# A two-layer selective scan on one core: first batch's softplus ahead of the last projections, dt out of PSUM ahead of the convolution

## The reference

```python
h = _layernorm(x) * (1 + ca) + sa
x = x + ga * attn(h)          # block 0: additive attention; block 1: two selective-scan layers
h = _layernorm(x) * (1 + cb) + sb
x = x + gb * ffn(h)           # block 0: FP4-quantised gated FFN; block 1: expert-choice mixture of experts
```

```python
xz = jnp.einsum('bld,ed->ble', x, W_in)
u, z = jnp.split(xz, 2, axis=-1)                     # 256 channels each
u = _silu(_causal_conv1d(u, conv_w, conv_b))         # 4 taps
x_dbl = jnp.einsum('bld,rd->blr', u, W_x)
dt, Bm, Cm = jnp.split(x_dbl, [8, 24], axis=-1)      # 8 | 16 | 16
dt = jax.nn.softplus(jnp.einsum('blr,dr->bld', dt, W_dt) + b_dt)
A = -jnp.exp(A_log)
y = _selective_scan(u, dt, A, Bm, Cm, Dvec)          # h = exp(dt A) h + dt B u, y = C h + D u, 16 states
y = y * _silu(z)
return jnp.einsum('bld,od->blo', y, W_out)
```

## Time and profile before

| what | value |
|---|---|
| median of 3 runs | 959.33 us (958.27 to 960.14) |
| profiled execution | 958.83 us, span 957.1 us |
| TensorE's mean granted clock | 0.831 of full |
| TensorE (PE) busy | 663.8 us, 69% |
| VectorE (DVE) busy | 677.4 us, 71% |
| ScalarE (ACT) busy | 439.1 us, 46% |
| GpSimd (POOL) busy | 567.0 us, 59% |
| decay Exp on ScalarE (L693), mean of one | 0.716 us |
| prologue of layer 0 | from 201.18 us (first projection) to 255.78 us (first scan) |
| prologue of layer 1 | from 485.19 us to 541.67 us |

### The profile page before, as it was taken

One profiled execution on the slowest core, in us unless ns is written; L12 is line 12 of the kernel. 1 busy time (PEld: TensorE's weight loads), 2 busy tenths in 40 slices (PEclk: granted clock), 3 DMA queues, 4 the chain that ended last, 5 costly groups with the idle time before them and its releaser, 6 DMA issues.

```text
span 957.1 us, 8556 instructions
## 1 busy us (share of the span) xinstructions
PE 663.8 (69%) x2416; PEld 337.7 (35%) x2416; DVE 677.4 (71%) x867; ACT 439.1 (46%) x715; POOL 567.0 (59%) x297
## 2 busy tenths in 40 slices
PE   3675576567377797878788386787978744299990
PEld 2344244432032232323322032232323224288880
DVE  6742477566598889899945598999998865844430
ACT  2413142257576465555556666465565513022220
POOL 6101564400399888999900399898998913136555
PEclk9755677688589899899997589899999975599995
DMA  4000000000000000000000000000000061012222
GB/s 154 0 1 1 0 1 0 1 0 0 1 0 0 1 0 0 0 0 0 0 1 0 1 0 1 0 0 1 0 0 0 0 241 44 1 12 19 20 21 22
DMA packets 11363, 13.05 MB, mean 14 GB/s; under 512 B 1545, under 2 KB 9914, under 8 KB 10690
## 3 DMA queue, kind: packets, MB, share of 16 engines
q1 hardware_dynamic: 6434, 10.51, 3.0%
q0 software_dynamic: 4896, 2.13, 2.6%
HBM read 8.43 MB, written 4.21 MB: 13 GB/s over the span
## 4 chain that ended last, share of the span: by engine, by line
PE 33%; DVE 29%; issue 14%; POOL 10%; ACT 9%; DMA 2%; DVEq 1%; POOLq 0%; ACTq 0%; SPq 0%
PE ps L924 7%; DVE ps L1302 6%; DVE hs_all L1315 6%; POOL hc_all L456 4%; PE ps L1050 3%; PE ps L1066 3%; PE ps L1027 2%; DVE w_ffn L1315 2%; PE ps L930 2%; ACT ps L693 2%; PE ps L886 2%; PE ps L769 1%; POOL dbu L443 1%; DVE big L1117 1%; DVE dbu L1349 1%
## 5 line engine op out<-in xcount | busy, mean ns | idle before, releaser
L924 PE MATMUL ps<-hc_all,ident 128*128 128x512 f32 x512 | 264.0, 640 | 21.6 <-POOL hc_all L456 20.4
L456 POOL TENSOR_TENSOR hc_all<-hs_all,c_row 128x1024 f32<-128x1024 f32 x88 | 210.5, 2392 | 19.4 <-DVE hs_all L1315 16.2
L690 ACT COPY c_row<-ps 128x512 f32<-128x512 f32 x128 | 74.9, 585 | 161.6 <-PE ps L943 145.9
L924 PEld LDWEIGHTS ps<-hc_all,ident 128*128 128x128 f32 x512 | 100.5, 201 | 119.1 <-issue 73.6
L1315 DVE TENSOR_TENSOR_SCAN hs_all<-da,ps 128x1024 f32<-128x1024 f32 x48 | 109.8, 2287 | 11.6 <-ACT da L693 5.4
L693 ACT ACTIVATE da<-big,a_neg 128x511 f32 (+1 forms) x176 | 117.2, 716 | 0.0
L1302 DVE TENSOR_TENSOR ps<-big,ps 128x1024 f32<-128x1024 f32 x88 | 107.4, 1220 | 11.7 <-POOL big L432 4.8
L456 POOL TENSOR_TENSOR hc_all<-w_ffn,c_row 128x1024 f32<-128x1024 f32 x40 | 94.2, 2356 | 22.1 <-DVE w_ffn L1315 22.1
L1315 DVE TENSOR_TENSOR_SCAN hs_all<-ps,dbu 128x1024 f32<-128x1024 f32 x40 | 91.0, 2274 | 12.4 <-POOL hc_all L456 9.7
L443 POOL TENSOR_TENSOR dbu<-big,w_mod 128x1024 f32<-128x1024 f32 x40 | 96.1, 2401 | 0.0
L1315 DVE TENSOR_TENSOR_SCAN w_ffn<-da,ps 128x1024 f32<-128x1024 f32 x40 | 91.5, 2287 | 5.3
(11 more groups left out here) (253 smaller groups left out, 1103.3 us busy)
## 6 DMA issues: line engine op xcount, KB each, us to landing
tmpA<-w_in SPq DMA_DIRECT2D x2, 1024.0 KB, 6.9
tmpB<-w_in SPq DMA_DIRECT2D x2, 1024.0 KB, 9.0
x_tok<-x_in SPq DMA_DIRECT2D x1, 1024.0 KB, 6.6
out<-x_tok SPq DMA_DIRECT2D x1, 1024.0 KB, 7.2
xm_rows<-xn SPq DMA_DIRECT2D x1, 1024.0 KB, 5.3
w_mod<-w_mod_in SPq DMA_DIRECT2D x1, 768.0 KB, 4.6
out<-hc_all,hs_all POOLq DMA_INDIRECT x40, 3.0
w_ffn<-w_ffn_in SPq DMA_DIRECT2D x1, 560.0 KB, 7.4
```

The source lines that it names most:

```text
L456: nc.gpsimd.tensor_tensor(hc[:, n % 4, :, :], hs3[HS_BUF[n]].rearrange("p (i s) -> p i s", i=IC), c_row[:, n % 4, :].unsqueeze(1).to_broad ...
L690: nc.scalar.copy(c_row[:, n % 4, :], ps[:, CB, :]).then_inc(c_cs, 1)
L924: mm = nc.tensor.matmul(ps[:, YS + i, :], ident[:], hc[:, n % 4, i, :], start=(n == 0), stop=(n == NS - 1))
```

## The change

The instructions and their shapes stay the same. Their order on three queues, the waits, and one bank pair change:

- VectorE: L1268 (dt out of PSUM) moves ahead of the convolution and counts `m_pos` for each half. In the last turn the sum of softplus of batch 0 (L1281) stands ahead of L1268 of batch 3.
- ScalarE: Abs (L659) moves ahead of z's Silu and waits half by half. In turn 4 the table load, A and Exp of batch 0 follow. In turn 5 Ln of batch 0 stands right after L629. The Silu load moves ahead of the hT writes (layer 0) and ahead of the last `store_h` of the layer before (layer 1).
- TensorE: batch 3's dt product goes into banks 0 and 1 and does not wait for Abs of batch 2. The waits ahead of the loop ask only for Abs of batches 0 to 2 and the rows of batch 0; the rest is asked for at state n = 3, ahead of the first product that writes banks 0 and 1. The first projection of layer 0 waits for two hT writes, and its z half for all four.

```diff
--- before.py
+++ after.py
@@ -168,7 +168,7 @@
         dtT = big[:, 0:IC * T].rearrange("p (b i s) -> p b i s", b=B, i=IC)
         dtuT = big[:, IC * T:2 * IC * T].rearrange("p (b i s) -> p b i s", b=B, i=IC)
         SP = S + KC - 1
-        XD, DTP = [4, 5], 6
+        XD, DTP = [4, 5], [6, 6, 6, 0]
         hs_all = sb("hs_all", [P, 2 * IC * S])
         hs = hs_all[:].rearrange("p (k i s) -> p k i s", k=2, i=IC)
         hc_all = sb("hc_all", [P, 4 * IC * S])
@@ -609,6 +609,7 @@
 
             act.wait_ge(stat_ready, 3 * NT)
             nc.scalar.activation(std[:], mv[:, :, 1], ACT.Sqrt, bias=eps[:, 0:1]).then_inc(std_ready, 1)
+            act.preload_act_table(ACT.Silu)
             for b in range(B):
                 act.wait_ge(norm_tr, B + b + 1)
                 nc.scalar.activation(hT[:, b * S:(b + 1) * S], ps[:, b, :], ACT.Identity, bias=mod_cols[:, 2, b:b + 1],
@@ -616,7 +617,14 @@
             for l in range(L):
                 q = sems[l]
 
-                act.preload_act_table(ACT.Silu)
+                def softplus_exp(b):
+                    act.wait_ge(q["m_abs"], b + 1)
+                    nc.scalar.activation(splus[:, b, :, :], splus[:, b, :, :], ACT.Exp, scale=-1.0).then_inc(q["m_ln"], 1)
+
+                def softplus_ln(b):
+                    act.wait_ge(q["m_ln"], 2 * b + 1)
+                    nc.scalar.activation(splus[:, b, :, :], splus[:, b, :, :], ACT.Ln, bias=1.0).then_inc(q["m_ln"], 1)
+
                 if l:
 
                     act.wait_ge(c_sum, NS * B)
@@ -627,6 +635,8 @@
                         after(act, q["m_dtp"], b - 2)
                         nc.scalar.copy(dt_low, ps[2 * NS:2 * NS + DR, XD[k], :]).then_inc(q["m_dtl"], 1)
                         nc.scalar.copy(bc_parts[0:2 * NS, b - 2, :], ps[0:2 * NS, XD[k], :]).then_inc(q["m_hi"], 1)
+                    if b == B + 1:
+                        softplus_ln(0)
                     if b < B:
 
                         act.wait_ge(q["m_in"], 2 * b + 1)
@@ -649,29 +659,24 @@
                             act.wait_ge(q["m_conv"], IC * (b - 1) + i + 1)
                             nc.scalar.activation(uT[:, b - 1, i, :], conv[:, (b - 1) % 2, i, :], ACT.Silu,
                                                  bias=vec(V_CB + l * IC + i)).then_inc(q["m_u"], 1)
+                    if b >= 2:
+
+                        for i in range(IC):
+                            act.wait_ge(q["m_pos"], IC * (b - 2) + i + 1)
+                            ins = nc.scalar.activation(splus[:, b - 2, i, :], ps[:, DTP[b - 2] + i, :], ACT.Abs,
+                                                       bias=vec(V_BDT + l * IC + i))
+                        ins.then_inc(q["m_abs"], 1)
                     if b < B:
                         act.wait_ge(q["m_in"], 2 * b + 2)
                         nc.scalar.activation(zT[:, b, :, :], ps[:, 2:4, :], ACT.Silu).then_inc(q["m_z"], 1)
-                    if b >= 2:
-
-                        act.wait_ge(q["m_pos"], b - 1)
-                        for i in range(IC):
-                            ins = nc.scalar.activation(splus[:, b - 2, i, :], ps[:, DTP + i, :], ACT.Abs,
-                                                       bias=vec(V_BDT + l * IC + i))
-                        ins.then_inc(q["m_abs"], 1)
-                act.preload_act_table_set("natural_log_exp_and_others")
-                if l == 0:
-
-                    nc.scalar.activation(a_neg[:].rearrange("p l i n -> p (l i n)"), vec(V_AL, L * IC * NS),
-                                         ACT.Exp).then_inc(a_exp, 1)
-
-                def softplus_log(b):
-                    act.wait_ge(q["m_abs"], b + 1)
-                    nc.scalar.activation(splus[:, b, :, :], splus[:, b, :, :], ACT.Exp, scale=-1.0).then_inc(q["m_ln"], 1)
-                    act.wait_ge(q["m_ln"], 2 * b + 1)
-                    nc.scalar.activation(splus[:, b, :, :], splus[:, b, :, :], ACT.Ln, bias=1.0).then_inc(q["m_ln"], 1)
-
-                softplus_log(0)
+                    if b == B:
+
+                        act.preload_act_table_set("natural_log_exp_and_others")
+                        if l == 0:
+                            nc.scalar.activation(a_neg[:].rearrange("p l i n -> p (l i n)"), vec(V_AL, L * IC * NS),
+                                                 ACT.Exp).then_inc(a_exp, 1)
+                        softplus_exp(0)
+
                 act.wait_ge(decay_zero, l + 2)
                 act.wait_ge(a_ready, 1)
                 def store_h(b):
@@ -700,7 +705,10 @@
                         if n == OUT_AT + 1 and not isinstance(b, int):
                             store_h(b)
                         if isinstance(b, int) and n + 2 in DT_AT:
-                            softplus_log(1 + DT_AT.index(n + 2))
+                            softplus_exp(1 + DT_AT.index(n + 2))
+                            softplus_ln(1 + DT_AT.index(n + 2))
+                if l + 1 < L:
+                    act.preload_act_table(ACT.Silu)
                 store_h(B)
 
             act.wait_ge(stat_ready, 4 * NT)
@@ -871,7 +879,6 @@
                     mm = nc.tensor.transpose(ps[:, b, j * P:(j + 1) * P], xn[:, b * TB + j, :], ident[:])
                 mm.then_inc(norm_tr, 1)
             pe.wait_ge(ld_mamba, 64)
-            pe.wait_ge(hT_ready, 2 * B)
             pe.wait_ge(consts, 7)
             for l in range(L):
                 q = sems[l]
@@ -881,6 +888,8 @@
 
                     if l:
                         pe.wait_ge(c_h, b + 1)
+                    elif b == 0:
+                        pe.wait_ge(hT_ready, B + 2 * (half + 1))
                     after(pe, q[["m_u0", "m_z"][half]], [2, 1][half] * b)
                     for i in range(IC):
                         mm = nc.tensor.matmul(ps[:, 2 * half + i, :], w_in[:, l, (2 * half + i) * P:(2 * half + i + 1) * P],
@@ -891,9 +900,10 @@
                 for b in range(B + 2):
                     if b >= 2:
                         pe.wait_ge(q["m_dtl"], b - 1)
-                        after(pe, q["m_abs"], b - 2)
+                        if b < B + 1:
+                            after(pe, q["m_abs"], b - 2)
                         for i in range(IC):
-                            mm = nc.tensor.matmul(ps[:, DTP + i, :], w_dt[:, l, i * P:(i + 1) * P], dt_low,
+                            mm = nc.tensor.matmul(ps[:, DTP[b - 2] + i, :], w_dt[:, l, i * P:(i + 1) * P], dt_low,
                                                   start=True, stop=True)
                         mm.then_inc(q["m_dtp"], 1)
                     if b < B:
@@ -909,8 +919,8 @@
                             mm = nc.tensor.matmul(ps[0:DR + 2 * NS, XD[(b - 1) % 2], :], w_x[:, l, i, :], uT[:, b - 1, i, :],
                                                   start=(i == 0), stop=(i == IC - 1))
                         mm.then_inc(q["m_xd"], 1)
-                pe.wait_ge(q["m_abs"], B)
-                pe.wait_ge(q["m_lo"], B)
+                pe.wait_ge(q["m_abs"], B - 1)
+                pe.wait_ge(q["m_lo"], 1)
 
                 def add_skip(b):
 
@@ -962,6 +972,9 @@
                         if n == LAG:
 
                             after(pe, c_y, l * B + b)
+                            if isinstance(b, int):
+                                pe.wait_ge(q["m_abs"], B)
+                                pe.wait_ge(q["m_lo"], B)
                         if n >= LAG:
                             add_state(at - LAG, n - LAG)
                         elif not isinstance(b, int):
@@ -1236,6 +1249,11 @@
             normalise(3)
             for l in range(L):
                 q = sems[l]
+                def softplus(b):
+                    dve.wait_ge(q["m_ln"], 2 * b + 2)
+                    dve.wait_ge(q["m_pos"], IC * (b + 1))
+                    v.tensor_tensor(dtT[:, b, :, :], dtT[:, b, :, :], splus[:, b, :, :], ALU.add).then_inc(q["m_dt"], 1)
+
                 if l:
                     dve.wait_ge(c_scan, B * NS)
                 v.memset(u_pad[:, :, :, 0:KC - 1], 0.0).then_inc(pad_ready, 1)
@@ -1247,6 +1265,15 @@
                         after(dve, q["m_lo"], b - 3)
                         v.tensor_tensor(bc_rest[:, k, :], ps[0:2 * NS, XD[k], :], bc_parts[0:2 * NS, b - 2, :],
                                         ALU.subtract).then_inc(q["m_r1"], 1)
+                        if b == B + 1:
+                            if l == 0:
+                                dve.wait_ge(a_exp, 1)
+                                v.tensor_scalar(a_neg[:], a_neg[:], -1.0, None, ALU.mult).then_inc(a_ready, 1)
+                            softplus(0)
+                        dve.wait_ge(q["m_dtp"], b - 1)
+                        for i in range(IC):
+                            v.tensor_scalar(dtT[:, b - 2, i, :], ps[:, DTP[b - 2] + i, :], vec(V_BDT + l * IC + i), 0.0,
+                                            ALU.add, ALU.max).then_inc(q["m_pos"], 1)
                     if b < B:
 
                         dve.wait_ge(q["m_u0"], 2 * b + 2)
```

(16 more changed lines are left out.)

## The result

The changed kernel takes 935.89 us (median of 4 runs, 934.05 to 936.44), the kernel before 959.44 in the runs beside it (4 runs, 958.27 to 960.14). The ratio is 0.9754, with a 95% interval of 0.9740 to 0.9769: 23.5 us faster. Predicted were 940.0 us and a range of 936 to 946.

The account below looks back on a forecast made before the run. Each prologue delays the whole span; ScalarE's queue, held by VectorE's, sets its turns, and its end is serial. Layer 0's 10.2 us (0.75 + 4.0 + 5.5) and layer 1's 9.3 sum to 19.5, giving 940 us, range 936 to 946.

Parts of the forecast that it names:

- Start: Start of each layer's prologue, earlier first projection and hoisted Silu load: 0.75 us won in layer 0, 0.1 in layer 1.
- the estimate was 1.5: Start of layer 1: at 2.66 us per table switch, the Silu hoist would bring about 1.5 us; not adopted.
- Turns: Prologue turns up to the last L628, dt ahead of the convolution: 4.0 us won in layer 0, 1.9 in layer 1.
- the falls of turns 2 and 3: Layer 1 prologue: TensorE at 1.2 GHz about 502 to 504 delays L909; turn 2 wins only 0.1 us.
- all at full clock: Case with TensorE at full clock and no contention: 21.4 us won, 938 us.
- Tail: Last L628 to first scan: 8.5 us instead of 14.0 in layer 0, 8.4 instead of 15.7 in layer 1.
- the two cases of the text: Prologue tail: L1272 stretched by GpSimd's product, or a slow last dt product without contention; both put layer 0's scan at 246.3.
- No table load was added: Abs under the Exp and Ln table: extra loads taken as 0, at most 5.1 us, total up to 945.
- the term for the loops: Scan loops: only their phase against the clock changes; 1 us either way allowed.
- A: Rival: TensorE at 1.2 GHz through the rest of both prologues, 12 us won in all, 947.5 us; chance 0.14.
- B: Rival: TensorE stays at 1.2 GHz into the loop and becomes the bound, slower than before, 984 us; chance 0.02.
- C: Rival: no change, decays wait for something equally late, memset near 252 as before, 959.3 us; chance 0.02.

Follow-up runs that it names:

- the shifted kernel: Changed kernel plus one idle VectorE memset (400 columns) ahead of the memset of the decay banks in layer 0: 936.05 us, ratio 0.9775.
- the kept-busy TensorE: Changed kernel plus idle matmuls in turn 4, two behind batch 2's dt product and two behind batch 3's product: 934.35 us, ratio 0.9765.
- upper group: Runs of the unchanged kernel before, the slower 51 of 64: 956.4 to 960.1 us.
- lower group: Runs of the unchanged kernel before, the faster 13 of 64: 953.3 to 954.8 us.

## Why the prediction was right, and where it was wrong

**Start.** From the normalisation's first instruction to the copy of u it is 203.52 - 191.10 = 12.42 us instead of 203.17 - 189.98 = 13.19: 0.77 won, 0.75 was forecast. The first projection of two hT writes ran partly at half clock (the pair took 4.02 us instead of the 3.67 of the earlier trace rows). In layer 1 0.14 instead of 0.1. From the Trainium skill's figure of 2.66 us for a table switch with its drain (ScalarE: Activation LUTs, What ACT_TABLE_LOAD costs) the estimate was 1.5; the trace does not agree, and again the load of Exp's set is followed by work 1.29 us behind its start (235.52, 236.81).

**Turns.** Layer 0: 238.07 - 213.87 = 24.20 us instead of 28.24, 4.04 won, 4.0 forecast. Layer 1, from 485.79: 26.11 instead of 28.22, 2.1 won, 1.9 forecast. That the last agrees so well is in part luck: the forecast took over the falls of turns 2 and 3, and the profiled execution had them. The changed kernel's second profile has 27.55 us there, 0.7 won, and that of the shifted kernel, without such a fall, 24.20, 4.0 won. So the 21.4 us given for "all at full clock", from which the lower end of the forecast came, were too few by some 2 us as well.

**Tail.** Layer 0: 246.59 - 238.07 = 8.52, forecast 8.5, where 14.02 had been. Layer 1: 520.41 - 511.90 = 8.51, forecast 8.4, where 15.69 had been. The last dt product was slow in both (3.78 and 3.77), one of the two cases of the text. L1294 then started 0.07 us behind the end of GpSimd's product and took 0.69, so that nothing was stretched in this execution. That the two cases give nearly the same end is what the kept-busy TensorE showed, to 0.2 us. No table load was added, so Abs runs under the table of Exp and Ln.

**The step that failed** is the term for the loops: "In the loops nothing changes but the phase at which they meet the clock: the three runs lie 1.9 us apart, I allow 1 either way." Layer 0's loop alone gave 2.64 us, and with layer 1's and the end it was 4.0, less 1.1 lost ahead of the prologues. The bound came from three runs that all lay in the upper group. Over its 64 runs the same kernel spans 6.8 us, and its profiles span 4.9 (957.1 and 952.2). With the first profile's loop I had a reference whose 226.31 us held 2.5 us that the same code needn't pay, and the stretches were in the trace: the rows of busy time from 330.9 and 385.5, with TensorE full at half clock. What they cost only a second profile could tell. The lower group of the kernel before less 19.5 us is 934 to 935, and there the lower end of the range had to be.

**The rivals.** A (half clock through both prologues) did not happen. In layer 0 of the profiled execution TensorE was at full clock from turn 2 until turn 4, which the smaller gaps had suggested; but the second profile of the same kernel has a fall in turn 3 (223.8 to 227.2), so the gaps do not settle it. In layer 1 it fell in turns 2 and 3 as before. B (the loop stays at half clock) did not happen. But its mechanism, TensorE as the bound while its clock is low, is the one at work in steps 5 to 7, and it worked against the kernel before. C fell: the memset moved from near 252 to 244.65.

## What to carry to other kernels

Where engines work in turns, look for the instruction that stands first in its consumer's need and last in its producer's queue. Here 1.4 us of VectorE behind a 4.07 us convolution set the turn of three engines, and a move of it within the queue, with the finer wait behind it, earned some 7 us without removing anything. The work of the first unit of the next phase can run in the gaps of the last unit's preparation, if it gets banks of its own; what is late next can be the cheapest instruction of the queue, here a memset. And before the reference of a sum is trusted, see whether its profile holds stretches in which a gated clock has made an engine the bound: such time may go without any doing of the change. One profile more of the reference, taken ahead of the forecast, can show it.

## What the runs showed of the hardware

The same program took 953.3 to 960.1 us on one core, in two groups, with TensorE's falls to 1.2 GHz in different places from execution to execution. A fall costs by what it meets: 1.57 and 1.34 us where it lasted into the output product, 0.07 where the clock rose ahead of that product, 0.02 at most for short falls at 112 and 184 us into the loop, 0.5 for a longer one at 58 us. The changed kernel, whose loop begins 9 us earlier, had none of the costly ones in three profiles. Why is open.

In the prologues a fall costs where a turn or the tail waits for TensorE: the second prologue of the changed kernel took 50.15, 51.60 and 50.14 us in three profiles, and 48.24 in the kernel that differs only by a memset in layer 0.

Abs of batch 3 behind the first decays made each prologue 0.7 us shorter. TensorE kept busy in turn 4 made each tail 0.2 us shorter, and its first prologue was 1.65 us longer. By their ratios, 0.9759 and 0.9765 beside 0.9762 of the changed kernel, neither can be told from it in the whole.
